# Scores ride with first halves, and three blocks' second halves are made after the maximum

## The chip, the core and the metric

The kernel runs on one core of a Trainium2 chip. That core has a matrix engine (TensorE, PE in the profile), three elementwise engines (VectorE or DVE, ScalarE or ACT, GpSimd or POOL), a queue engine (SyncE or SP) and 16 DMA engines. Each engine runs its own instruction list in order, and waits on semaphores for the others. The metric is device time in microseconds (us), lower is better.

## The reference, cut to what matters

Two graph layers over 2048 rows of 512 features, each followed by a residual and a layer norm. The first layer adds `adj @ x` with a few corrections for pairs of rows. The second is the one the change touches:

```python
seq = (x @ W_seq).reshape(N, 16, 32)                  # N = 2048, 16 heads of 32
score1 = einsum('nhd,d->hn', seq, a1)
score2 = einsum('nhd,d->hn', seq, a2)
scores = leaky_relu(score1[:, :, None] + score2[:, None, :], 0.2)
attn   = softmax(scores + (1 - adj) * -65500, axis=-1)
hidden = einsum('hij,jhd->ihd', attn, seq).reshape(N, 512)
x      = layernorm(x + elu(hidden @ W_out + b_out))
```

`adj` has some five ones in a row, so the softmax is taken over gathered neighbours only. It is made stable with one bound for each head: the largest `score2` of all 2048 rows.

## The kernel before

Rows are tiled into 16 blocks of 128 (`NB` = 16). The whole program is written out by hand, engine by engine; nothing reorders it. What runs when is set by the order in each engine's list and by semaphores.

**First stage (up to about 157 us).** The adjacency rows are read, cast, turned and multiplied with x.

**Middle stage (157 to 231 us).** For each block b, in a software pipeline over the engines: ScalarE lays `x * scale` in a PSUM bank (`scale_x`), TensorE adds the pair correction (`correct`), VectorE sums and measures the row (`sum_rows`), ScalarE takes the root, VectorE normalizes (`norm_rows`), TensorE turns the block (`turn_x1`), ScalarE saves it (`save_xT`), and TensorE multiplies it with W_seq in two halves (`make_seq`, L867). Each half is 256 columns of seq and 16 columns of scores: score1 (`s1`) with the first half, score2 (`s2`) with the second. ScalarE saves them (`save_seq`, L1140 the half, L1142 the scores), and SyncE stores the finished block of seq and s2 into the table `seqtab` in HBM (L491). Beside this, `spread_keys`, `save_keys` and `pick_edges` make for each row a list of up to four neighbours (`eidx`) and `one_hots` (L1915) the squares that place gathered rows.

**The turn (231 to 241 us).** With all 16 blocks' scores saved, VectorE reduces s2 to a maximum (L1967), TensorE turns it (L956), VectorE reduces and lays it on a diagonal (L1970, L1971), TensorE spreads it to all partitions (L959), and VectorE copies it out (L1976). Then come VectorE's instructions for the node's own weight and the bound (L2017 to L2043), and the first block's `arguments` (L2049 to L2057).

**Last stage (237 to 385 us).** For each block, GpSimd gathers 5 rows a node from `seqtab` (L616: one `near` and four `eidx`, 128 rows of 528 numbers each), VectorE makes the exponents' arguments, ScalarE takes Relu and Exp (L1257, L1259), VectorE lays the node's own share (`own_share`, L1999), weighs the gathered rows (`weigh`, L2080), TensorE adds them up (L985), VectorE divides (`finish`, L2010, L2012), TensorE turns and projects with W_out (L885, L894), ScalarE and VectorE do the elu, the residual and the last norm.

**What orders the gathers.** The gather's four buffers (`GR` = 4) hold one block each. GpSimd starts when the first 13 blocks (`CUT` = 13) are in the table (semaphore `tab_first`). For the first three blocks (`EARLY` = 3) the edges are sorted so that four gathers need only these 13 blocks (semaphore `e_low`) and the fifth needs the whole table (`e_high`). GpSimd's list is: 12 low gathers, wait for the whole table (`tab_store`), 3 high gathers, then 5 gathers for each of blocks 3 to 15, from block 4 on after TensorE has released the buffer (`e_agg`).

## Time and profile before

| | us |
|---|---|
| median of 3 runs (lowest, highest) | 387.03 (386.94, 387.91) |
| the profiled execution | 387.15 |
| its span, first to last instruction | 385.4 |
| busy in the span: PE, DVE, ACT, POOL | 346.7, 324.0, 201.2, 183.8 |
| mean granted TensorE clock | 0.971 |

The profiled execution's own time is 1.75 us more than its span, and 0.12 us above the median. PE is busy for 90% of the span and DVE for 84%, but these are means: PE holds the time up to 231 us, and DVE is busy in 19.3 of 20 us in the stretches after 280 us. Line numbers are those of the kernel before.

### The profile page before, as it was taken

Reading aid. Unit: us, or ns where it says so; the run is one execution under the profiler, and the core shown is the slowest. Engines: PE = TensorE matmul, PEld = TensorE weight load, DVE = VectorE, ACT = ScalarE, POOL = GpSimd, SP = SyncE. Lnnn points to the kernel's source line nnn. Section 1 sums busy time; section 2 is a strip of 40 time slices with the busy share of each in tenths; the row PEclk is TensorE's granted clock in tenths of the full one; section 3 lists DMA queues with packets and bytes.
Section 4 is the critical chain, followed back from the end, with each engine's and each line's share of the span. In section 5 each row is a group of like instructions: output and inputs, shape, how many; then the busy total and the mean of one; then the engine's idle time right before and its main releaser. Section 6 shows DMA issues by size and latency. Waiting matters only on the chain.

```text
span 385.4 us, 5301 instructions
## 1 busy us (share of the span) xinstructions
PE 346.7 (90%) x1676; PEld 218.5 (57%) x1676; DVE 324.0 (84%) x846; ACT 201.2 (52%) x453; POOL 183.8 (48%) x178
## 2 busy tenths in 40 slices
PE   0899899999999989999999992999999999999870
PEld 0444555455444454578888871786676555665540
DVE  2999999997797758777888868998999999999772
ACT  3955876545632013465555432132457776677780
POOL 7775738777773100000000077687788888750000
PEclk9999999999999999999999996699999999999995
DMA  7999553345898210681121178666666776760014
GB/s 247 371 384 381 211 189 142 112 140 170 201 228 193 95 70 0 201 321 56 57 77 66 58 192 260 193 167 169 188 184 169 205 216 194 193 191 36 27 58 145
DMA packets 34758, 65.11 MB, mean 169 GB/s; under 512 B 15648, under 2 KB 16800, under 8 KB 32672
## 3 DMA queue, kind: packets, MB, share of 16 engines
q1 hardware_dynamic: 25632, 42.45, 32.8%
q0 software_dynamic: 9088, 22.20, 21.6%
q8 instruction: 17, 0.28, 0.3%
q14 instruction: 21, 0.17, 0.1%
HBM read 53.50 MB, written 8.52 MB: 161 GB/s over the span
## 4 chain that ended last, share of the span: by engine, by line
PE 43%; DVE 36%; ACT 5%; issue 5%; POOL 5%; DMA 4%; SPq 0%; DVEq 0%; ACTq 0%; POOLq 0%
PE ps L867 14%; PE ps L664 14%; DVE adjT L2080 8%; PE ps L985 5%; POOL pr L546 5%; DMA arenaA<-in_x_dram 3%; DVE arenaC L1948 2%; DVE stage L1946 2%; DVE ps L2006 2%; DVE ps L1999 2%; DVE arenaA L2012 2%; DVE arenaB L1349 2%; PE ps L856 2%; DVE arenaB L1915 2%; PE ps L646 1%
## 5 line engine op out<-in xcount | busy, mean ns | idle before, releaser
L664 PE MATMUL ps<-arenaB,adjT 128*128 128x512 f16 x512 | 116.9, 384 | 3.1 <-ACT adjT L1045 1.9
L546 POOL DMA_INDIRECT pr<-in_adj_dram,aidx x79 | 82.2, 1040 | 32.1 <-issue 22.4
L616 POOL DMA_INDIRECT adjT<-seqtab,eidx x64 | 80.0, 1250 | 19.5 <-issue 19.5
L664 PEld LDWEIGHTS ps<-arenaB,adjT 128*128 128x128 f16 x512 | 49.6, 99 | 60.7 <-issue 4.0
L985 PE MATMUL ps<-adjT,arenaB 128*128 128x264 f32 x256 | 63.7, 398 | 1.7 <-DVE adjT L2080 1.1
L616 POOL DMA_INDIRECT adjT<-seqtab,near x16 | 15.8, 987 | 97.4 <-DMA seqtab<-arenaA 91.8
L867 PE MATMUL ps<-stage 128*128 128x272 f32 x256 | 61.5, 393 | 0.1
L985 PEld LDWEIGHTS ps<-adjT,arenaB 128*128 128x128 f32 x256 | 49.3, 196 | 18.6 <-DVE adjT L2080 5.0
L894 PE MATMUL ps<-adjT 128*128 128x512 f32 x120 | 54.0, 592 | 0.0
L867 PEld LDWEIGHTS ps<-stage 128*128 128x128 f32 x256 | 47.4, 190 | 9.4 <-ACT stage L1134 0.6
L2080 DVE TENSOR_TENSOR adjT<-adjT 128x1024 f32<-128x1024 f32 (+2 forms) x37 | 47.8, 1307 | 0.3
L1036 ACT ACTIVATE halves<-stage 128x2048 f16<-128x2048 f32 x16 | 30.8, 1923 | 14.1 <-DVE deg L1380 6.6
L894 PEld LDWEIGHTS ps<-adjT 128*128 128x128 f32 x120 | 21.6, 190 | 21.5 <-issue 21.5
L1045 ACT COPY adjT<-ps 128x1024 f16<-128x1024 f16 x20 | 19.2, 1014 | 22.7 <-PE ps L646 22.7
L1354 DVE TENSOR_TENSOR arenaA<-iota,halves 128x2048 f16<-128x2048 f16 x15 | 18.3, 1222 | 5.4 <-ACT halves L1036 5.2
L646 PE MATMUL ps<-identh,halves 128*128 128x128 f16 x176 | 13.3, 236 | 9.6 <-ACT halves L1036 9.6
L1361 DVE MAX8 arenaA<-arenaA 128x8 f16<-128x256 f16 x60 | 21.1, 414 | 0.5
L1366 DVE MAX8 arenaA<-arenaA 128x8 f16<-128x256 f16 x60 | 20.8, 409 | 0.0
L1165 ACT COPY ps<-adjT 128x512 f32<-128x512 f32 x15 | 8.9, 591 | 22.0 <-DVE stage L1946 22.0
L1140 ACT COPY arenaA<-ps 128x256 f32<-128x256 f32 x32 | 12.0, 375 | 14.4 <-PE ps L867 14.4
L646 PEld LDWEIGHTS ps<-identh,halves 128*128 128x128 f16 x176 | 12.0, 106 | 12.0 <-issue 9.1
L1257 ACT ACTIVATE stage<-stage 128x80 f32<-128x80 f32 (+2 forms) x19 | 4.8, 253 | 24.8 <-DVE stage L2057 24.8
(302 smaller groups left out, 501.9 us busy)
## 6 DMA issues: line engine op xcount, KB each, us to landing
stage<-in_adj_dram SPq DMA_DIRECT2D x16, 1024.0 KB, 5.4
seqtab<-arenaA SPq DMA_DIRECT2D x16, 264.0 KB, 2.3
arenaA<-in_x_dram SPq DMA_DIRECT2D x4, 1024.0 KB, 13.2
out_dram<-arenaC SPq DMA_DIRECT2D x16, 256.0 KB, 3.5
arenaB<-in_x_dram SPq DMA_DIRECT2D x1, 1536.0 KB, 10.6
pr<-in_adj_dram,aidx POOLq DMA_INDIRECT x79
arenaC<-in_L_gnn_Wq_dram SPq DMA_DIRECT2D x1, 1024.0 KB, 16.6
arenaC<-in_L_gnn_Wk_dram SPq DMA_DIRECT2D x1, 1024.0 KB, 19.7
```

What stands on the lines that cost most here:

```text
L546: g.indirect_dma_start(out=avals[:, t:t + 1], out_offset=None, in_=adj_flat, in_offset=bass.IndirectOffsetOnAxis(ap=aidx[:, t:t + 1], axis ...
L616: g.indirect_dma_start(out=Grow[:, b % GR, k, :], out_offset=None, in_=table, in_offset=bass.IndirectOffsetOnAxis(ap=source, axis=0)).then ...
L646: ins = t.transpose(turn_banks(b)[:, j, :], arowh[:, b % 2, j * P:(j + 1) * P], identh[:])
L664: ins = t.matmul(bank(4 + b % 2), adjT[:, b, j, :], xsplit[:, w, j, :], start=(j == 0 and w == 0), stop=(j == NB - 1 and w == 1))
L867: ins = t.matmul(half_bank(n), xT[:, b % 2, k, :], Wx[:, k, s, :], start=(k == 0), stop=(k == KT - 1))
L894: ins = t.matmul(bank(6 + b % 2), hT[:, b % 2, k, :], Wo[:, k, :], start=False, stop=(k == KT - 1), skip_group_check=True)
L985: ins = t.matmul(bank(2 * (b % 2) + c, HALF), square, Grow[:, b % GR, k, c * HALF:(c + 1) * HALF], start=False, stop=(k == GE - 1), skip_g ...
L1036: s.activation(arowh[:, b % 2, :], arow[:, b % 2, :], ACT.Identity, accum_out=deg[:, 0, b:b + 1]).then_inc(row_cast, 1)
L1045: s.copy(adjT[:, b, 8 * k:8 * k + 8, :], turn_banks(b)[:, 8 * k:8 * k + 8, :]).then_inc(row_evac, 1)
L1361: v.max(top[:, 0, 8 * k:8 * k + 8], key[:, k * SEG:(k + 1) * SEG])
L1366: ins = v.max(top[:, 0, 8 * k:8 * k + 8], key[:, k * SEG:(k + 1) * SEG])
L2080: v.tensor_tensor(some[:, :, 0:D1], some[:, :, 0:D1], some[:, :, D1:HW].to_broadcast([P, (last - first) * H1, D1]), ALU.mult).then_inc(e_m ...
```

## The change

Nothing is computed otherwise; what moves is where and when. Both score columns sit in the first half's product, which grows from 272 to 288 columns; the second half shrinks from 272 to 256. ScalarE writes the 16-bit copy of s1 (`ek`) that VectorE wrote. `sum_rows` and `correct` of a block run up to two blocks further ahead of `make_seq`. Blocks 13, 14 and 15 make their first halves one after another, and their second halves (`make_half(..., 1)`) follow, mixed with the maximum's small products. `EARLY` is 2, so that 8 low gathers stand ahead of the wait for the whole table instead of 12. The last stage begins with the low parts of blocks 0 and 1, then their high parts.

```diff
-    EARLY = 3
+    EARLY = 2
+        PARTS = [(0, 0, KE), (1, 0, KE), (0, KE, GE), (1, KE, GE)] + [(b, 0, GE) for b in range(EARLY, NB)]
...
+        def nth_half(b, k):
+            return 2 * b + k if b < CUT else 2 * CUT + k * (NB - CUT) + b - CUT
+        def keys_bank(b):
+            return ps[:, 4, 256:256 + KE * KW] if b == NB - 2 else ps[:, 7, 0:KE * KW]
+        def summed_in(b):
+            return {0: (2,), 1: (3,), 2: (4, 5), 3: (6,), 4: (7, 8)}.get(b, (b + 4,) if b + 4 < NB else ())
+        def normed_in(b):
+            return {0: (1,), 1: (2,), 2: (3,), 3: (4, 5), 4: (6,), 5: (7, 8)}.get(b, (b + 3,) if b + 3 < NB else ())
...
             for b in range(NB):
-                sp.wait_ge(seq_saved, 2 * b + 2)
-                sp.wait_ge(s12_saved, 2 * b + 2)
+                sp.wait_ge(seq_saved, nth_half(b, 1) + 1)
+                sp.wait_ge(s12_saved, 3 * b + 3)
                 sp.dma_start(seqtab[b * P:(b + 1) * P, :], rows_of[:, b, :]).then_inc(tab_first if b < CUT else tab_store, 16)
...
+            def make_half(b, half, lo=0, hi=KT):
+                n = nth_half(b, half)
+                pe.wait_ge(x_evac, b + 1)
+                if n >= 3:
+                    pe.wait_ge(seq_saved, n - 2)
+                cols = slice(SC + D // 2, SC + D) if half else slice(0, SC + D // 2)
+                for k in range(lo, hi):
+                    ins = t.matmul(half_bank(b, half), xT_of(b)[:, k, :], Wx[:, k, cols], start=(k == 0),
+                                   stop=(k == KT - 1))
...
+            def save_half(b, k):
+                act.wait_ge(seq_made, nth_half(b, k) + 1)
+                made = half_bank(b, k)
+                if k == 0:
+                    s.copy(s1[:, b, :], made[:, 0:H1]).then_inc(s12_saved, 1)
+                    s.copy(ek[:, b, 18:18 + H1], made[:, 0:H1]).then_inc(s12_saved, 1)
+                    s.copy(s2[:, b, :], made[:, H1:SC]).then_inc(s12_saved, 1)
+                    made = made[:, SC:]
+                s.copy(seq[:, b, 8 * k:8 * k + 8, 0:D1], made.rearrange("p (h d) -> p h d", h=8)).then_inc(seq_saved, 1)
...
+            def save_last():
+                save_half(CUT + 2, 1)
+                save_keys(CUT + 1)
+                save_keys(CUT + 2)
...
                         if n == 1:
+                            act.wait_ge(tab_first, 16 * CUT)
+                            s.copy(s2[:, 0:CUT], ones[:, 0:1].unsqueeze(1).to_broadcast([P, CUT, H1])).then_inc(self_exp, 1)
                             act.wait_ge(self_made, 1)
                             s.activation(sa[:, 2], sa[:, 1], ACT.Exp).then_inc(self_exp, 1)
+                            save_last()
+                        if b == 4:
+                            table_stored(act)
+                            s.copy(s2[:, CUT:], ones[:, 0:1].unsqueeze(1).to_broadcast([P, NB - CUT, H1])).then_inc(self_exp, 1)
...
+                    dve.wait_ge(e_low[0], 16 * KE)
+                    arguments(0, 0, KE)
+                    self_rest()
+                    one_hots(3)
+                    self_parts()
+                    own_share(0)
+                    weigh(0, 0, KE)
+                    dve.wait_ge(e_low[1], 16 * KE)
+                    arguments(1, 0, KE)
+                    own_share(1)
+                    weigh(1, 0, KE)
+                    dve.wait_ge(e_high[0], 16)
+                    arguments(0, KE, GE)
+                    one_hots(4)
+                    weigh(0, KE, GE)
+                    dve.wait_ge(e_high[1], 16)
+                    arguments(1, KE, GE)
+                    one_hots(5)
+                    weigh(1, KE, GE)
+                    finish(0)
```

TensorE's list at the end of the middle stage, before. L867 is a half of seq (4 products), L877 the keys, L956 and L959 the maximum, L929 a product that opens a PSUM bank:

```order
L867 MATMUL ps<-stage 128x272 [waits s12_saved,x_evac]
L867 MATMUL ps<-stage 128x272 x3
L867 MATMUL ps<-stage 128x272 [waits s12_saved]
L867 MATMUL ps<-stage 128x272 x3
L877 MATMUL ps<-ekb,stage 128x51 [waits keys_saved,s1_split,span_made]
L877 MATMUL ps<-ekb,stage 128x51 x3
L877 MATMUL ps<-ekb,stage 128x51 [waits keys_saved,s1_split,span_made]
L877 MATMUL ps<-ekb,stage 128x51 x3
L956 MATMUL ps<-ident,gm 16x128 [waits g_part]
L959 MATMUL ps<-gm,ones 128x16 [waits keys_saved,g_diag]
```

And now, from the middle of block 13's second half (L887 a half, L904 the keys, L989 and L993 the maximum, L956 a bank):

```order
L989 MATMUL ps<-ident,gm 16x128 [waits g_part]
L887 MATMUL ps<-stage 128x256 [waits seq_saved,x_evac]
L887 MATMUL ps<-stage 128x256
L887 MATMUL ps<-stage,halves 128x256 [waits seq_saved,x_evac]
L993 MATMUL ps<-gm,ones 128x16 [waits g_diag]
L887 MATMUL ps<-stage,halves 128x256 [waits seq_saved,x_evac]
L887 MATMUL ps<-stage,halves 128x256 x2
L904 MATMUL ps<-ekb,stage 128x51 [waits keys_saved,s1_split,span_made]
L904 MATMUL ps<-ekb,stage 128x51 x3
L956 MATMUL ps<-iota,identh 128x512 x2
L887 MATMUL ps<-stage 128x256 [waits seq_saved,x_evac]
```

Both products of the maximum stood behind all halves; now ten of the twelve products of the last three second halves stand behind the first of them, and block 15's second half stands last.

ScalarE's list at the turn, before (L1142 the last scores, L1150 keys, L1257 and L1259 the first block's Relu and Exp):

```order
L1142 COPY arenaA<-ps 128x16
L1150 CAST halves<-ps 128x204 [waits keys_spread] x2
L296 TENSOR_LOAD badi [waits flag_made]
L296 ISA x2
L1248 COMPARE_AND_BRANCH
L1249 ACT_TABLE_LOAD
L1257 ACTIVATE stage<-stage 128x64 [waits e_arg]
L1259 ACTIVATE adjT<-stage 128x64 [waits e_cap]
L1262 ACTIVATE arenaB<-arenaB 128x256 [waits self_made]
```

And now (L1191 a half of seq, L1203 keys, L1328 and L1330 Relu and Exp):

```order
L1308 ACT_TABLE_LOAD
L1191 COPY arenaA<-ps 128x8x32 [waits seq_made] x2
L1203 CAST halves<-ps 128x204 [waits keys_spread]
L296 TENSOR_LOAD badi [waits flag_made]
L296 ISA x2
L1321 COMPARE_AND_BRANCH
L1328 ACTIVATE arenaB<-arenaB 128x64 [waits e_arg]
L1330 ACTIVATE adjT<-arenaB 128x64 [waits e_cap]
L1333 COPY arenaA<-ones 128x208 [waits tab_first]
L1335 ACTIVATE arenaB<-arenaB 128x256 [waits self_made]
L1191 COPY arenaA<-ps 128x8x32 [waits seq_made]
L1203 CAST halves<-ps 128x204 [waits keys_spread] x2
```

The copy of block 15's second half, on which the last store to the table waits, stood ahead of the first block's Relu; now it stands behind that block's Exp, a fill of ones and the own weights' Exp.

## Rows read from the trace of the kernel before

**Rows 1.** The chain of waits, 225 to 275 us: start us, length us, what.
```profile
231.23 0.60 DVE gm L1967
...
241.21 7.51 PE ps L985 x20
...
249.16 4.45 PE ps L985 x20
...
262.37 4.45 PE ps L985 x20
```

**Rows 2.** TensorE in order of time: start us, length us, engine, line.
```profile
213.69 0.38 PE L848 MATMUL ps<-scores,arenaA 128*128 128x512 f16 x1
213.91 0.60 PE L856 MATMUL ps<-ident,arenaC 128*128 128x128 f32 x4
214.34 3.83 PE L867 MATMUL ps<-stage 128*128 128x272 f32 x16
218.01 0.26 PE L877 MATMUL ps<-ekb,stage 128*128 128x51 f16 x4
```

**Rows 3.** ScalarE in order of time, from the last stores to the first weights.
```profile
218.21 0.37 ACT L1140 COPY arenaA<-ps 128x256 f32<-128x256 f32 x1 [0.69 <-PE ps L867]
218.48 0.19 ACT L1142 COPY arenaA<-ps 128x16 f32<-128x16 f32 x1
...
237.51 0.26 ACT L1257 ACTIVATE stage<-stage 128x64 f32<-128x64 f32 x1 [3.74 <-DVE stage L2057]
237.80 0.32 ACT L1259 ACTIVATE adjT<-stage 128x64 f32<-128x64 f32 x1
238.18 0.42 ACT L1262 ACTIVATE arenaB<-arenaB 128x256 f32<-128x256 f32 x1
```

**Rows 4.** GpSimd in order of time; in brackets the idle time before and its releaser.
```profile
222.27 0.95 POOL L616 DMA_INDIRECT adjT<-seqtab,near  x1 [91.77 <-DMA seqtab<-arenaA]
...
232.51 0.94 POOL L616 DMA_INDIRECT adjT<-seqtab,near  x1 [0.30 <-issue]
...
249.49 0.95 POOL L616 DMA_INDIRECT adjT<-seqtab,near  x1 [1.35 <-PE ps L985]
...
253.51 1.97 POOL L616 DMA_INDIRECT adjT<-seqtab,eidx  x1 [0.31 <-issue]
...
263.42 0.94 POOL L616 DMA_INDIRECT adjT<-seqtab,eidx  x1 [0.30 <-issue]
```

**Rows 5.** VectorE in order of time; L2049 begins a block's arguments.
```profile
229.71 0.42 DVE L1910 TENSOR_TENSOR arenaB<-halves 128x256 f32<-128x256 f16 x1
...
236.70 0.27 DVE L2049 TENSOR_TENSOR stage<-arenaB,adjT 128x64 f32<-128x64 f32 x1
...
256.58 0.29 DVE L2049 TENSOR_TENSOR stage<-arenaB,adjT 128x80 f32<-128x80 f32 x1
...
262.64 0.30 DVE L2049 TENSOR_TENSOR stage<-arenaB,adjT 128x80 f32<-128x80 f32 x1
...
269.07 0.69 DVE L1946 SCALAR_TENSOR_TENSOR stage<-ps,adjT 128x512 f32<-128x512 f32 x1 [1.08 <-ACT adjT L1176]
...
270.41 0.29 DVE L2049 TENSOR_TENSOR stage<-arenaB,adjT 128x80 f32<-128x80 f32 x1
...
280.15 0.29 DVE L2049 TENSOR_TENSOR stage<-arenaB,adjT 128x80 f32<-128x80 f32 x1
```

**Rows 6.** Line L616, 236 to 270 us: the gathers' landing.
```profile
DMA to landing us min/median/max: 3.4/4.0/4.8
```

**Rows 7.** Line L491, 200 to 222 us, then 226 to 236 us: the stores' landing.
```profile
DMA to landing us min/median/max: 2.0/2.0/2.8
...
DMA to landing us min/median/max: 4.0/4.1/4.3
```

**Rows 8.** Stretches: length; busy us of PE, PEld, DVE, ACT, POOL; granted clock; DMA share.
```profile
233.00:234.00 1.00, 1.00 (x5) 0.48 (x5) 0.75 (x3) 0.77 (x1) 0.70 (x2) 0.64 0.89 340
...
247.00:248.00 1.00, 1.00 (x6) 0.86 (x5) 1.00 (x2) 0.00 (x0) 0.85 (x1) 1.00 0.75 199
```

More of the change, by code:

```diff
@@ L313, in table_stored, with lots_of @@
             eng.wait_ge(tab_store, 16 * (NB - CUT))
-        def lots_of(b):
-            if b == 0:
-                return tuple((k, k + 1) for k in range(GE))
-            return ((0, 2), (2, KE), (KE, GE)) if b < EARLY else ((0, 2), (2, GE))
+        def lots_of(b, lo):
+            if b >= EARLY:
+                return ((0, 2), (2, GE))
+            if lo:
+                return ((KE, GE),)
+            return ((0, 2), (2, KE)) if b else tuple((k, k + 1) for k in range(KE))
+        LOTS = [(b, first, last) for b, lo, hi in PARTS for first, last in lots_of(b, lo)]
         def weighed(b, k):
-            before_b = sum(len(lots_of(a)) for a in range(b))
-            return before_b + 1 + [lo <= k < hi for lo, hi in lots_of(b)].index(True)
+            return [a == b and first <= k < last for a, first, last in LOTS].index(True) + 1
         def bank(n, width=512):
@@ L357, in two_layer_graph_attention @@
         x1 = ax
-        HC = D // 2 + H1
-        Wx = part(stage, 0, [KT, 2, HC])
+        SC = 2 * H1
+        Wx = part(stage, 0, [KT, SC + D])
         xT = part(stage, 2304, [2, KT, P])
+        xT_late = part(halves, 1408, [KT, P])
         eT = part(arenaB, 0, [2, N])
@@ L383, in two_layer_graph_attention @@
         mxe = part(arenaB, NB * GE * H1, [NB, GE * H1])
-        span = part(stage, 3328, [2, KE * P], F16)
+        span = part(stage, 3328, [3, KE * P], F16)
         spare = adjbuf
@@ L388, in two_layer_graph_attention @@
         ehot = part(arenaB, 3840, [HOTS, KE, P])
-        earg = part(stage, 2 * KE * P, [3, GE * H1])
+        earg = part(arenaB, 3840 + HOTS * KE * P, [3, GE * H1])
         sden = sb("sden", [P, 2, H1])
@@ L966, in pe_second_layer @@
                 with pe.If(misfit < 1):
[L967 to L968 removed]
+                    for b, lo, hi in PARTS:
+                        if (b, lo) == (0, KE):
+                            pe.wait_ge(keys_saved, NB)
                             open_bank(6)
@@ L1228, in act_first_norm @@
                 scale_x(2)
-                for b in range(NB):
-                    if b + 3 < NB:
-                        scale_x(b + 3)
+                for b in range(CUT):
+                    ahead = summed_in(b + 1)
+                    late = b in (2, 4)
+                    if not late:
+                        for c in ahead[0:1]:
+                            scale_x(c)
                     if b == 0:
                         save_xT(0)
-                    if b + 1 < NB:
-                        root(b + 1)
+                    for c in normed_in(b):
+                        root(c)
                     if b >= 1:
                         save_xT(b)
-                    if b >= 1:
                         save_seq(b - 1)
@@ L2075, in weigh @@
                         dve.wait_ge(e_exp, nth_part(b, lo))
-                        for first, last in lots_of(b):
-                            if not lo <= first < hi:
-                                continue
+                        for first, last in lots_of(b, lo):
                             some = G[:, b % GR, first * H1:last * H1]
```

230 lines of the change are left out of this document (120 added, 110 removed).

## The prediction, made before the changed kernel was run

> **What bounds the kernel now.** I read the chain of waits first, because it says which engine holds the time at each stage. Up to 231 us it lies on TensorE, whose blocks follow each other without a gap. At 231.23 us VectorE's maximum takes over. From 241.21 us the chain shows TensorE's sums, twenty products in 7.51 us where later blocks take 4.45 [rows 1]. After 269 us it lies on VectorE to the end.
>
> Then I read VectorE in order of time for that last part. The first arguments start at 236.70 us, block 3's at 256.58, block 4's at 262.64, block 5's at 270.41 and block 6's at 280.15. The only idle time of note is 1.08 us at 269.07 [rows 5]. So today the last part is VectorE's own work, 33.7 us from the first arguments to block 5's.
>
> Last I read GpSimd, which nobody seems to wait for. It starts at 222.27 us, its ninth gather starts at 232.51, so one takes 10.24 / 8 = 1.28 us, and the last gather of block 5 starts at 263.42 [rows 4]. A gather lands 4.0 us after its issue in this stretch (3.4 to 4.8) [rows 6]. So block 5 is complete at about 267.4 us and VectorE asks for it at 270.41. The slack is only 3.0 us, and that number decides this change.
>
> **The maximum, and with it the last stage, starts earlier.** Two halves of a block take 218.01 - 214.34 = 3.67 us, a correction 0.22 (213.69 to 213.91) and a turn 0.43 (213.91 to 214.34), starts compared [rows 2]. Block 12 ended at 218.01. Now one more correction and one more turn lie ahead of its end, +0.65: 218.66. Block 15's turn and two key products follow (0.43 + 2 x 0.10), then three first halves of 288 columns, each 3.67 x 288 / 544 = 1.94 us. They end at 225.1. ScalarE's copy started 0.2 us after the product (218.21 against 218.01) and three small copies take some 0.4, from 0.19 each and overlapping [rows 3]. With VectorE's last 16-column maximum it is 225.9 us, where it was 231.83 (231.23 + 0.60) [rows 1].
>
> From there to the first arguments it took 236.70 - 231.83 = 4.87 us. Now VectorE has four small instructions of the neighbour list and the keys ahead, 0.17 to 0.42 us each as at 229.71 [rows 5], some 0.9 in all, and the two small products queue behind two or three products of a second half, for which I add 0.4. That makes 6.2 us: first arguments at 232.1, 4.6 us earlier. The extra cast on ScalarE (0.19 each) has cover, since ScalarE waits for TensorE in every block (0.69 at 218.21 [rows 3]). The fill of ones leaves VectorE for ScalarE; on VectorE it was hidden behind ScalarE's Exp, so I count nothing for it there. `sum_rows` run ahead cost VectorE nothing in total; they fill it earlier. Without that cover, TensorE would stand in the middle stage, which is a rival below.
>
> **The gathers start a little later and then stand.** Block 12's store went out after 218.67 (218.48 + 0.19), and GpSimd started at 222.27, 3.6 us later [rows 3, 4]. Now its half is saved at 218.66 + 0.2 + 0.37 = 219.23, and without a score copy behind it counts at once. GpSimd starts at 222.8, about 0.5 later. Eight gathers end its free work at 233.0. The ninth waits for the whole table, and that waits for block 15's second half.
>
> TensorE has that half ready at about 232.5: from 225.1 three second halves of 1.73 (3.67 x 256 / 544) give 5.2, two opened banks 0.9, the rest is small products and the wait for the diagonal. But ScalarE takes it only after the first block's Exp. Before, the Relu started 0.81 us after the arguments, the Exp 0.29 later and the own weights' Exp 0.38 after that, ending 1.90 after the arguments' start [rows 3, 5]. With the fill of ones between (0.3, a copy of less width than the Exp's 0.42) and a half's 0.27 to 0.37, the half is saved at 232.1 + 1.9 + 0.3 + 0.3 = 234.6. Add the 3.6 of block 12's store: GpSimd goes on at 238.2 us. It has stood 5.2 us. The ninth gather was at 232.51, so it is 5.7 us late. Stores land in 2.0 to 2.8 us there and in 4.0 to 4.3 beside gathers [rows 7], so the 3.6 may be 0.8 too much or 2.3 too little.
>
> GpSimd gets back 1.05 us: before block 4 it waited 1.35 for TensorE where the ordinary step is 0.30 [rows 4], and TensorE will be done with block 0 by then. So block 5's last gather is 5.7 - 1.05 = 4.6 us late.
>
> **The sum.** VectorE alone would ask for block 5 at 232.1 + 33.7 - 1.08 = 264.7, 5.7 us earlier than today. But the gather lands at 263.42 + 4.6 + 4.0 = 272.0, which is 1.6 us later than the 270.41 of today. The 4.6 us gained at the turn are waited away: first 3 to 4 us at block 2, whose fifth gather starts six steps of 1.28 after 238.2 and lands at 249.9, while VectorE is there by about 246 (232.1, and 13.8 for two blocks: the 19.9 from 236.70 to 256.58 for three, less the 6.1 of one); the rest at blocks 3 to 5. Behind block 5 VectorE bounds again, since block 6 was asked for only at 280.15, 9.7 us later, and GpSimd needs some 7.5 a block (below). So 1.6 us stays to the end: 387.15 + 1.6 = 388.75 us for the profiled execution, which was 0.12 above the median of the runs. I say 388.6.
>
> One unknown is how long a gather takes beside VectorE. The gather at 253.51 took 1.97 us instead of 0.95 [rows 4], while VectorE weighed block 2. The ten gathers of blocks 4 and 5 took from 249.49 to 264.36, 14.9 us or 7.5 a block, where ten steps of 0.95 + 0.30 are 12.5. Between none of this and twice this lies -2.4 to +2.4 at block 5; I take the same as today, because the same weighing of blocks 2 to 4 falls on the same gathers.
>
> The landing is the other term with weight. The Trainium skill (DMA: Bandwidth & Descriptors, "Anatomy of one DMA") fits a transfer issued from GpSimd as 2.0 us plus bytes over 436 GB/s. For 270 KB that would be an estimated 2.6 us, and block 5 would be complete 1.4 us earlier, which leaves 0.2 us of loss. No gather of this stretch lands under 3.4 [rows 6], so the measurement decides.
>
> **The rivals.** (a) Faster, 385.2 us. The gathers catch up. VectorE idles some 5 us between blocks 1 and 5, and GpSimd's steps in that time are clean 1.25s. For it: the clean steps before 236 us. Against it: every weighing still takes place while gathers run. Price: 238.2 + 21 x 1.25 = 264.5, landed at 268.5, a gain of 1.9: 387.15 - 1.9 = 385.25, or 385.1 on the median's scale. It decides for faster as soon as block 5's last gather starts before 265.2 us, a gain of more than 1.2. The Trainium skill (SBUF — State Buffer, "SBUF: two separate sides") speaks for this rival: GpSimd's descriptor writing is locked out only while a VectorE instruction holds the port pair they share, so a waiting VectorE stretches nothing. The trace agrees as far as the 1.97 goes; no run shows yet how much of the stretch the waits remove.
>
> (b) No change, 387.0 us. ScalarE or the store is 1.6 us quicker than I have it, for instance a store that lands in 2.0 us because GpSimd's queue is empty. For it: 2.0 in the quiet stretch. Against: block 12's 3.6 us were already quiet.
>
> (c) Slower still, 390.8 us. TensorE becomes the second bound. Its clock fell at 233.0 to 234.0 (0.64 granted on average, on the way from 2.4 to 1.2 GHz) when it had little to do, and was back at 247.0 [rows 8], so block 0 and its neighbours took 7.51 instead of 4.45. If the wait for block 2 makes it fall again, block 2's sums run slow, 3 us late. I work out that they end near 260, block 3's at 268.5, while VectorE wants these at about 269: covered by half a microsecond. If not covered, or if the corrections run ahead make TensorE stand earlier, it is 2 us more.
>
> (d) That the change doesn't do what it says: the maximum still ends near 231, because the first halves wait for banks. Then nothing is gained at the turn, and the store is later by the same amount: about 389 to 392. I give it little.
>
> **How the numbers follow.** Forecast 0.55, (a) 0.20, (b) 0.15, (c) and (d) 0.10. What can't be told from no change is 0.3%, 1.2 us. The forecast's own range is 387.3 to 389.9, with half of the gathers' stretch and of the store's bounds. Faster: (a) and a little of (b), 0.22. Same: most of (b) and 0.07 of the forecast, 0.20. Slower: 0.58. The range reaches from 385.3 to 390.6.
>
> **What would show it.** In the profile after: first halves ahead of the maximum and VectorE's first arguments near 232 (right if 231 to 233.5). GpSimd idle for 4 to 6 us before its ninth gather, released by the stores, ending near 238. VectorE idle about 3 us before block 2's arguments and some more at blocks 3 to 5, released by gathers. Block 5's arguments near 272, and from there on the same distances as before, 9.7 us to block 6. ScalarE's copy of the last half near 234.5. The prediction is wrong if GpSimd's idle time is under 3 us, if VectorE does not wait for block 5, or if block 5's arguments start before 270.4.

## The result: 0.2 to 0.45% slower, and the profile after

The changed kernel took 388.23 us (median of 20 runs, 386.55 to 391.7) against 386.94 for the kernel before: a ratio of 1.0045, 95% interval 1.003 to 1.0059. A second series gave 387.89 and 1.0017 (0.9997 to 1.0037), which alone would not tell it from no change, and the kernel before against itself 0.9999 (0.9979 to 1.0019). The forecast was 388.6. The profiled execution took 388.47 us, its span 386.7.

The two profiled executions can't be laid over each other by their clocks, because the stage ahead of the projection ended 1.7 us earlier in one. So I count from the first product of the projection. In the rows of before it is this one (timeline: start, us, engine, line), and then the one of after:

```profile
160.37 3.94 PE L867 MATMUL ps<-stage 128*128 128x272 f32 x16
```

```profile
158.69 3.50 PE L887 MATMUL ps<-stage 128*128 128x288 f32 x14
```

From here on "at 70.0" means 70.0 us behind that product. The kernel before, profiled a second time, shows how well this repeats: first arguments at 76.33 both times, block 5's at 110.04 and 110.15, block 6's at 119.78 and 119.85.

VectorE of after, in order of time, answers to [rows 5]:

```profile
224.00 0.19 DVE L2028 TENSOR_TENSOR gm<-gm,arenaA 128x16 f32<-128x16 f32 x1 [0.84 <-ACT arenaA L1189]
...
228.71 0.27 DVE L2139 TENSOR_TENSOR arenaB<-arenaB,adjT 128x64 f32<-128x64 f32 x1
...
235.37 0.28 DVE L2139 TENSOR_TENSOR arenaB<-arenaB,adjT 128x64 f32<-128x64 f32 x1 [1.01 <-DMA adjT<-seqtab,eidx]
...
239.98 0.19 DVE L2139 TENSOR_TENSOR arenaB<-arenaB,adjT 128x16 f32<-128x16 f32 x1 [0.79 <-DMA adjT<-seqtab,eidx]
...
249.13 0.30 DVE L2139 TENSOR_TENSOR arenaB<-arenaB,adjT 128x80 f32<-128x80 f32 x1 [4.62 <-DMA adjT<-seqtab,eidx]
...
255.87 0.31 DVE L2139 TENSOR_TENSOR arenaB<-arenaB,adjT 128x80 f32<-128x80 f32 x1 [1.35 <-DMA adjT<-seqtab,eidx]
...
262.61 0.30 DVE L2139 TENSOR_TENSOR arenaB<-arenaB,adjT 128x80 f32<-128x80 f32 x1 [0.58 <-DMA adjT<-seqtab,eidx]
...
269.89 0.69 DVE L2036 SCALAR_TENSOR_TENSOR stage<-ps,adjT 128x512 f32<-128x512 f32 x1 [1.30 <-ACT adjT L1229]
...
271.23 0.30 DVE L2139 TENSOR_TENSOR arenaB<-arenaB,adjT 128x80 f32<-128x80 f32 x1
...
280.93 0.29 DVE L2139 TENSOR_TENSOR arenaB<-arenaB,adjT 128x80 f32<-128x80 f32 x1
```

The maximum is done at 224.19 (65.5), and the first arguments start at 70.0, where they were at 76.3: the turn came 6.3 us forward. Then the waits for gathers eat it: 1.01 us ahead of block 1's low part, 0.79 ahead of block 0's high part, 4.62 at block 2, 1.35 at block 3, 0.58 at block 4. The first of these is not from GpSimd standing, since block 1's low gathers are issued before it stands, and the second profile below doesn't have it. Block 5's arguments are at 112.5 and block 6's at 122.2, 2.4 us later than before.

GpSimd of after answers to [rows 4]:

```profile
220.22 0.94 POOL L636 DMA_INDIRECT adjT<-seqtab,near  x1 [91.41 <-DMA seqtab<-arenaA]
...
229.58 1.07 POOL L636 DMA_INDIRECT adjT<-seqtab,eidx  x1 [0.30 <-issue]
236.32 1.27 POOL L636 DMA_INDIRECT adjT<-seqtab,eidx  x1 [5.67 <-DMA seqtab<-arenaA]
...
244.74 0.95 POOL L636 DMA_INDIRECT adjT<-seqtab,eidx  x1 [0.31 <-issue]
...
265.51 2.50 POOL L636 DMA_INDIRECT adjT<-seqtab,eidx  x1 [0.30 <-issue]
```

It starts at 61.5 (before 61.9) and stands 5.67 us ahead of its ninth gather. The last row is block 5's last gather, at 106.8. It landed 5.6 us later, at 112.4, just ahead of block 5's arguments at 112.5. ScalarE of after answers to [rows 3]; the fifth row is the last half's save:

```profile
229.53 0.26 ACT L1328 ACTIVATE arenaB<-arenaB 128x64 f32<-128x64 f32 x1 [1.20 <-DVE arenaB L2147]
229.82 0.32 ACT L1330 ACTIVATE adjT<-arenaB 128x64 f32<-128x64 f32 x1
229.98 0.55 ACT L1333 COPY arenaA<-ones 128x208 f32<-128x208 f32 x1
230.32 0.42 ACT L1335 ACTIVATE arenaB<-arenaB 128x256 f32<-128x256 f32 x1
230.64 0.36 ACT L1191 COPY arenaA<-ps 128x256 f32<-128x256 f32 x1
```

And the chain of waits of after shows what lies behind the save, where [rows 1] had the maximum:

```profile
231.03 5.03 DMA seqtab<-arenaA
...
236.32 1.27 POOL adjT L636
...
244.74 4.36 DMA adjT<-seqtab,eidx
...
252.10 7.15 PE ps L1027 x20
```

TensorE stood 6.77 us ahead of block 2's sums, and its granted clock went to the lower of its two levels (0.50 of 2.4 GHz, so 1.2), as in [rows 8]. The twenty products took 7.15 us. The windows of after (PE, PEld, DVE, ACT, POOL busy, clock, DMA share, GB/s):

```profile
248.00:250.00 2.00, 0.00 (x0) 0.00 (x0) 0.80 (x4) 0.00 (x0) 1.39 (x3) 1.00 0.73 222
250.00:252.00 2.00, 0.00 (x0) 0.00 (x0) 1.92 (x4) 1.52 (x4) 1.70 (x2) 0.56 0.82 220
252.00:254.00 2.00, 1.90 (x5) 1.52 (x6) 1.97 (x3) 0.00 (x0) 1.70 (x2) 0.50 0.44 156
258.00:260.00 2.00, 2.00 (x12) 1.55 (x11) 2.00 (x2) 0.28 (x1) 1.39 (x3) 1.00 0.79 220
```

### The profile page after: what moved, and what is told of

Its sections match the earlier page's. It is cut to its first block, busy times and chain, and to the rows that moved or that the text cites. A ratio compares the mean times of both kernels' runs of the same rounds, so it can differ in the third digit from the quotient of the medians.

```text
span 386.7 us, 5313 instructions
## 1 busy us (share of the span) xinstructions
PE 347.4 (90%) x1676; PEld 219.0 (57%) x1676; DVE 319.8 (83%) x823; ACT 201.8 (52%) x469; POOL 184.2 (48%) x178
## 4 chain that ended last, share of the span: by engine, by line
DVE 36%; PE 33%; POOL 10%; issue 7%; DMA 6%; ACT 5%; SPq 0%; DVEq 0%; ACTq 0%; POOLq 0%
PE ps L887 13%; POOL pr L566 9%; DVE adjT L2166 8%; PE ps L684 8%; PE ps L1027 3%; DVE arenaB L1427 3%; DMA arenaA<-in_x_dram 3%; DVE arenaC L2038 2%; DVE stage L2036 2%; DVE ps L2096 2%; DVE arenaA L2102 2%; DVE ps L2089 2%; PE ps L876 2%; DVE arenaB L1992 2%; POOL adjT L636 1%
## 5 line engine op out<-in xcount | busy, mean ns | idle before, releaser
L636 POOL DMA_INDIRECT adjT<-seqtab,eidx x64 | 76.2, 1190 | 24.9 <-issue 19.2
L1027 PE MATMUL ps<-adjT,arenaB 128*128 128x264 f32 x256 | 65.0, 403 | 2.2 <-DVE adjT L2166 1.5
L636 POOL DMA_INDIRECT adjT<-seqtab,near x16 | 20.6, 1288 | 96.0 <-DMA seqtab<-arenaA 91.4
L887 PE MATMUL ps<-stage 128*128 128x288 f32 (+1 forms) x240 | 58.0, 393 | 0.1
L887 PEld LDWEIGHTS ps<-stage 128*128 128x128 f32 x240 | 44.3, 190 | 9.2 <-ACT stage L1180 0.6
L1328 ACT ACTIVATE arenaB<-arenaB 128x80 f32<-128x80 f32 (+2 forms) x18 | 4.6, 255 | 28.3 <-DVE arenaB L2147 28.3
L1191 ACT COPY arenaA<-ps 128x256 f32<-128x256 f32 x32 | 12.1, 393 | 10.8 <-PE ps L887 10.8
```

What stands on the lines that cost most here:

```text
L636: g.indirect_dma_start(out=Grow[:, b % GR, k, :], out_offset=None, in_=table, in_offset=bass.IndirectOffsetOnAxis(ap=source, axis=0)).then ...
L887: ins = t.matmul(half_bank(b, half), xT_of(b)[:, k, :], Wx[:, k, cols], start=(k == 0), stop=(k == KT - 1))
L1027: ins = t.matmul(bank(2 * (b % 2) + c, HALF), square, Grow[:, b % GR, k, c * HALF:(c + 1) * HALF], start=False, stop=(k == GE - 1), skip_g ...
```

## The experiments

Twelve runs, of 6 to 12 executions each. The table has the medians, the ratio to the kernel before, and from the profile the start of block 5's and block 6's arguments behind the first product. That start tells smaller effects apart than the median does, whose ratio is known to 0.2 or 0.3%. But each position comes from one or two profiled executions, and where a gather sets it, it moves with that gather's landing, by 0.3 us between the two profiles of the changed kernel.

```
                                      median   ratio (95%)             block 5   block 6
before, first profile                 386.94   -                       110.04    119.78
before again                          386.73   0.9999 (0.9979-1.0019)  110.15    119.85
changed                               388.23   1.0045 (1.003-1.0059)   112.54    122.24
changed again                         387.89   1.0017 (0.9997-1.0037)  112.23    121.94
before, two split                     387.95   1.0030 (1.001-1.0049)   110.39    120.08
before, two split, again              387.46   1.0018 (1.000-1.0035)   110.50    120.20
changed, three split                  384.45   0.9930 (0.9911-0.9948)  109.63    119.32
changed, last half first              387.93   1.0032 (1.0004-1.006)   111.44    121.13
changed, late half                    387.98   1.0032 (1.0008-1.0056)  111.70    121.40
changed, busy                         386.76   1.0004 (0.9985-1.0024)  111.33    121.02
three split + last half first         384.34   0.9950 (0.9924-0.9976)  108.20    117.90
the same, two gathers fewer           383.87   0.9917 (0.9886-0.9948)  108.10    117.84
the same, busy                        384.32   0.9941 (0.9917-0.9965)  108.04    117.75
the same, busy, two gathers fewer     383.24   0.9901 (0.987-0.9932)   106.48    116.21
```

**Three split blocks in the changed kernel.**

```diff
-    EARLY = 2
+    EARLY = 3
-PARTS = [(0, 0, KE), (1, 0, KE), (0, KE, GE), (1, KE, GE)] + [...]
+PARTS = [(0, 0, KE), (1, 0, KE), (2, 0, KE), (0, KE, GE), (1, KE, GE), (2, KE, GE)] + [...]
+SUMMED = [(0, 0, KE), (1, 0, KE), (0, KE, GE), (1, KE, GE), (2, 0, KE), (2, KE, GE)] + [...]  # TensorE
...
+                    dve.wait_ge(e_low[2], 16 * KE)
+                    arguments(2, 0, KE)
+                    weigh(2, 0, KE)
...
```

> The changed kernel, with the gathers of block 2 split as well, as they were before the change: twelve gathers of low rows stand ahead of GpSimd's wait for the whole table instead of eight, and block 2's low part is weighed before the high parts of blocks 0 and 1. Theory T (the loss comes from GpSimd standing for the whole table behind only eight gathers): four more gathers of 1.28 us fill 5.1 of the 5.67 us; GpSimd idles under 1 us there, VectorE's 4.62 us wait ahead of block 2 goes, block 5 is asked for some 4 us earlier, and the time is about 384 us, 0.8% under the kernel before (3 us), 4 under the changed one. Rival M (the new middle stage, or the order of the parts, costs what is gained): the time stays at 387.5 to 388.5. Rival V (VectorE's own work is the bound from block 3 on and the wait was covered): within 1 us of the changed kernel.

Measured: 384.45 us, 0.7% under the kernel before. So theory T holds in its main point and both M and V fall: the early scores do pay, once GpSimd has work in front of its wait. Block 5 came 2.9 us earlier, where T had said 4. GpSimd still idles 2.23 us, not under 1, because the last store now lands in 6.80 us (chain, then GpSimd's and VectorE's timeline):

```profile
231.19 6.80 DMA seqtab<-arenaA
```

```profile
238.26 1.95 POOL L638 DMA_INDIRECT adjT<-seqtab,eidx  x1 [2.23 <-DMA seqtab<-arenaA]
```

```profile
239.93 0.27 DVE L2141 TENSOR_TENSOR arenaB<-arenaB,adjT 128x64 f32<-128x64 f32 x1 [0.54 <-DMA adjT<-seqtab,eidx]
...
254.03 0.30 DVE L2141 TENSOR_TENSOR arenaB<-arenaB,adjT 128x80 f32<-128x80 f32 x1 [2.04 <-DMA adjT<-seqtab,eidx]
...
268.51 0.30 DVE L2141 TENSOR_TENSOR arenaB<-arenaB,adjT 128x80 f32<-128x80 f32 x1 [1.25 <-DMA adjT<-seqtab,eidx]
```

Of the wait ahead of block 2 0.54 us is left. A wait of 2.04 us stands ahead of block 3, and block 5 now waits for its own gather, 1.25 us.

**The kernel before with two split blocks**, twice.

```diff
-    EARLY = 3
+    EARLY = 2
...                                  # one_hots stay with the blocks they were with
```

> The kernel before, with only the number of split blocks taken from 3 to 2; the scores, the maximum and the parts stand where they stood. Theory T: GpSimd's eight gathers end at 232.5 us, the last store lands near 235, so GpSimd stands some 2.5 to 3 us; it had 3.0 us of slack at block 5 and gets 1.05 back at block 4, and the first arguments stay at 236.7. So the time is that of the kernel before to within 0.5 us (386.6 to 387.6): the split alone costs next to nothing, and only beside the earlier maximum is it the limit. Rival S (fewer split blocks cost by themselves, about as much as the whole change): 388.3 or more. Rival C (the lower instruction count of VectorE for block 2 helps): 386 or less.

> The kernel before with only two split blocks, once more: its median was 1.003 of the kernel before (1.001 to 1.0049), while its profile put block 6's arguments only 0.3 us later than the kernel before does, counted from the projection's first product (120.08 against 119.78 and 119.85). If the trace is right and the first series was high by chance, the ratio is 1.000 to 1.002 and block 6 stands at 120.0 to 120.4 again. If fewer split blocks cost 1 us by themselves, the ratio is 1.002 to 1.004, and the second profile shows VectorE's wait for block 4's gathers (1.89 us in the first) longer, block 6 at 120.8 or more.

GpSimd stood 3.09 and 3.24 us, as T has it, and block 5 came 0.3 to 0.4 us later:

```profile
236.51 0.96 POOL L616 DMA_INDIRECT adjT<-seqtab,eidx  x1 [3.24 <-DMA seqtab<-arenaA]
```

```profile
265.39 0.32 DVE L2049 TENSOR_TENSOR stage<-arenaB,adjT 128x80 f32<-128x80 f32 x1 [1.95 <-DMA adjT<-seqtab,eidx]
```

Block 6 came at 120.08 and 120.20, the second inside the 120.0 to 120.4 of "the trace is right"; VectorE's wait for block 4's gathers was 1.89 and 1.95 us, so it did not grow. The medians say more, 1.3 and 0.6 us against the runs of before in the same series, and T's 386.6 to 387.6 missed the first. Some 0.35 us of both lies outside the span: a run of this kernel takes 2.18 and 2.15 us more than its span (medians), one of the kernel before 1.81. Why is open, and so is the rest of the first. So the split alone costs 0.3 us by the trace and 0.6 to 1.3 by the clock. With the early scores it costs 2.9 at block 6 (122.24 against 119.32) and some 3.6 us of time. The two parts of the change are not additive: the early scores without the smaller split gain 2.2 us (384.45 against 386.66 in the same series), the smaller split alone loses 0.6 to 1.3, both together lose 1.0 to 1.3.

One thing in these profiles bears on the whole case. Block 5's last gather starts at 106.5 here, where the changed kernel has it at 106.8 and 106.0. Here it landed in 3.9 us, at 110.4, and there in 5.6 and 6.25. So at block 5 the changed kernel is no longer behind in when it issues that gather, but in how long that gather takes.

**The last half first.**

```diff
+                make_half(CUT + 2, 1)          # behind block 14's, ahead of keys and banks
                 spread_keys(CUT)
...
-                make_half(CUT + 2, 1)
...
                 save_half(CUT + 1, 1)
+                save_half(CUT + 2, 1)          # was behind the first Exp
                 save_keys(CUT)
...
-                save_half(CUT + 2, 1)
```

> The changed kernel, with block 15's second half made right behind block 14's on TensorE (ahead of the keys and two opened banks) and saved by ScalarE ahead of the first Relu, not behind the first Exp, the fill of ones and the own weights' Exp. Theory T: the half is saved 1.2 to 1.7 us earlier, GpSimd's idle time falls from 5.67 to about 4.3 us, and the gathers and VectorE's wait ahead of block 2 follow one for one; block 5 is not set by its gather any more in the changed kernel's trace, so the end moves by 1 to 1.5 us: about 387.0. Rival V (the wait is covered by VectorE's own bound): 388.2, unchanged. Rival M (moving keys and banks costs at the first arguments): slower than the changed kernel.

The half was saved 1.2 us earlier, GpSimd's idle time fell to 3.50 us, and block 6 came 1.1 us earlier than in the first profile of the changed kernel, 0.8 earlier than in the second:

```profile
234.49 1.44 POOL L636 DMA_INDIRECT adjT<-seqtab,eidx  x1 [3.50 <-DMA seqtab<-arenaA]
```

The sign is T's. But the gathers did not follow one for one: the ninth came 2.2 us earlier than in the first profile (75.5 against 77.6), block 5's last only 0.4 (106.4 against 106.8). The median moved by 0.3 us only, which the noise covers, so by the time nothing is shown. The changed kernel's second profile, with 4.63 us of idle time and nothing changed, shows how far the store's landing varies by itself.

**The last half late.**

```diff
+    s.copy(zt.rearrange("p a d -> p (a d)"), iota[:, 0:2 * D]).then_inc(opened_late, 1)
+    s.copy(ze.rearrange("p a d -> p (a d)"), iota[:, 0:2 * D]).then_inc(opened_late, 1)
+    act.wait_ge(opened_late, 2)
     save_last()
```

> The changed kernel, with two copies of 1024 columns into unused scratch on ScalarE ahead of block 15's last save: some 2 us more before the last store, and nothing else of that stage waits for them. Theory T: GpSimd stands 7.7 us instead of 5.67, VectorE waits 2 us longer ahead of block 2, and the time is 1.7 to 2.2 us more than the changed kernel's, about 390.2. Rival V: under 0.5 us more. It gives the slope of the end against the stall, together with the kernel that saves the half early.

T failed here. The save came 2.0 us later (235.41 in a run whose first product was at 161.43, so 74.0, where it was 72.0), but GpSimd went on at 77.2 instead of 77.6:

```profile
235.41 0.37 ACT L1192 COPY arenaA<-ps 128x256 f32<-128x256 f32 x1
```

```profile
238.64 1.26 POOL L637 DMA_INDIRECT adjT<-seqtab,eidx  x1 [5.23 <-DMA seqtab<-arenaA]
```

The last store landed in 2.6 us instead of 5.03. (The expectation under "Three split, last half first" calls it 2.9, which was the median of the last three stores.) In the changed kernel's two profiles and the busy kernel's below it was issued at 72.3 each time and landed at 77.4, 76.3 and 76.1; issued at 74.4 here, it landed at 77.0, and at 71.2 with the last half first, at 75.2. So the save 2 us later brought the landing no later than the changed kernel's own spread. This fits a store that waits behind the data of the eight gathers just ahead of it: with 2.4 us for them to drain it took half of 5.03. No run looked at the store's own data, so that reason is argued and not shown. Rival V's "under 0.5 us more" came out, though not by V's cause: the stall that the edit was to lengthen did not grow.

**TensorE kept busy** in its gap ahead of block 2's sums.

```diff
...
     turn_hidden(b - 2)
+    if b == 2:
+        for _ in range(28):
+            t.matmul(bank(5), identh[:], iota[:, 0:512], start=True, stop=True)
...
```

> The changed kernel, with 28 more products of 512 columns on TensorE into a bank that nobody reads, behind the turn of block 0's hidden rows, in the gap in which TensorE waits for block 2 (6.77 us there). They keep the granted clock at its upper level and leave all else where it stands. Theory C (the part of the loss that GpSimd's wait does not explain is TensorE's clock, which falls to the lower level in this gap: block 2's twenty sums take 7.15 us instead of 4.45 and the elu of block 0, for which VectorE waits 1.30 us ahead of block 5, is late by that): block 2's sums take some 4.5 us, the wait of 1.30 goes, block 5 is asked for at about 111.2 us behind the first product of the sequence's projection instead of 112.54, and the time falls by 1.0 to 1.5 us to about 387. Rival G (block 5's gather, which ended its landing just before, sets it anyway): at most 0.4 us.

```profile
244.29 6.21 PE L1018 MATMUL ps<-iota,identh 128*128 128x512 f16 x28
250.83 1.13 PE L1030 MATMUL ps<-adjT,ident 128*128 128x264 f32 x4 [0.33 <-DVE adjT L2169]
251.80 3.72 PE L1030 MATMUL ps<-adjT,arenaB 128*128 128x264 f32 x16
```

The sums took 4.69 us (250.83 to 255.52), the wait for the elu is gone, block 5 came at 111.33 and the median was 386.76: the numbers are theory C's. Shown is that GpSimd's wait makes the gap, that the clock falls in it, and that unused products hold it up. That the gain at block 5 comes from the clock is not shown. In both profiles of the changed kernel block 5's last gather landed at 112.4 and 112.2, so without the wait for the elu VectorE would have waited for that gather to within 0.1 us of the same time. In the busy kernel the gather started at 106.5 and landed in 4.5 us, at 111.0; what set block 5 there was VectorE's own work behind its wait at block 4:

```profile
262.97 0.30 DVE L2142 TENSOR_TENSOR arenaB<-arenaB,adjT 128x80 f32<-128x80 f32 x1 [2.57 <-DMA adjT<-seqtab,eidx]
```

And the two kernels with slow sums whose gather landed in 5.0 and 4.7 us, last half first and late half, had block 5 at 111.44 and 111.70 without any busy products. So rival G's mechanism, the gather, stands beside C's, and this run can't tell them apart.

**Three split, last half first.** Both edits from above.

> The kernel with three split blocks, and block 15's second half made right behind block 14's and saved ahead of the first Relu. Theory Q (the last store is held up behind the data of the gathers issued ahead of it: it landed in 2.9 us when issued last, 5.0 behind eight gathers, 6.8 with twelve): issued 1 us earlier, with fewer gathers ahead of it, it lands some 2 us earlier, so that GpSimd's 2.23 us of idle time ahead of its 13th gather goes to under 1 and block 5, which is set by its own gather there, is asked for 1 to 1.5 us earlier: about 383.3 us, under the kernel with three split blocks (384.45). Rival F (what the store gains, the gathers that share the DMA engines with it lose): no change against that kernel, 384.4.

The store landed in 4.0 us and GpSimd does not idle at all between its first gather and block 6. Block 5 came 1.4 us earlier than with three split alone, as Q said; the median, 384.34 against 384.45, doesn't show it, and Q's 383.3 was missed. In the three kernels below, whose store is issued at the same place, it landed in 5.1, 5.2 and 3.7 us, so a part of what it gained against 6.80 is the landing's own spread.

**Two gathers fewer, and TensorE busy, on that kernel.**

```diff
-                    for k in range(GE):
+                    for k in range(b in (4, 5), GE):      # two gathers fewer
                         gather(b, k, e_gather[b % GR])
...
-                        dve.wait_ge(e_gather[b % GR], 16 * GE * ((b - EARLY) // GR + 1))
+                        dve.wait_ge(e_gather[b % GR], 16 * (GE * ((b - EARLY) // GR + 1) - (b % GR < 2)))
...
                             open_bank(7)
+                            for _ in range(12):           # busy
+                                t.matmul(bank(5), identh[:], iota[:, 0:512], start=True, stop=True)
```

> The kernel before this in the list (three split blocks, last half first), which leaves out the gathers of the nearest neighbours of blocks 4 and 5 (two of GpSimd's gathers; their slots keep old rows, VectorE's and TensorE's work is the same). Theory G (from the first arguments on, GpSimd's gathers set when block 5 can be weighed, not VectorE): block 5's last gather starts 2.5 us earlier and lands 2.5 earlier, block 5 is asked for earlier by what VectorE waits for gathers at blocks 4 and 5, 1 to 1.6 us, and the end moves by the same: some 382.2. Rival V (VectorE's own work): no change, under 0.3 us.

> The kernel with three split blocks and the last half first, with twelve more products on TensorE into an unread bank ahead of the high parts' sums, where TensorE stands 3.06 us and its clock then runs at the lower level for some 4 us (in the trace of the kernel with three split blocks). Theory C: the eight sums behind it take 2 us instead of 3.85 and GpSimd's next slots come free earlier, but block 5 is set by its gather and not by TensorE: within 0.4 us of the same kernel without them. If the clock mattered there, 1 us less.

> Three split blocks, last half first, the twelve products that keep TensorE's clock up, and the gathers of the nearest neighbours of blocks 4 and 5 left out. Each of the last two by itself left block 5's arguments at 108.0 to 108.1 us behind the first product: without the two gathers VectorE waited 1.30 us for the elu of block 0, behind TensorE's slow sums; with the products it waited 1.35 for its gather. Theory D (two bounds stand one behind the other, gathers and TensorE, at the same place): both together give 1 to 1.3 us, arguments at 106.8 to 107.1, and some 383 us. Rival V (VectorE's own work stands right behind both): under 0.4 us.

The kernels with fewer gathers leave out two neighbours and so compute something else; they only price the gathers. Alone, neither edit moved block 5: 108.20 became 108.10 and 108.04. G's 1 to 1.6 us was wrong, though its first half held: block 5's last gather started 2.9 us earlier (100.8 against 103.7), although GpSimd stood 2.19 us for block 4's buffer, which TensorE had to release. What VectorE waited for changed, as its rows show, of the kernel with fewer gathers, of the busy one, and of the one with both:

```profile
267.39 0.69 DVE L2038 SCALAR_TENSOR_TENSOR stage<-ps,adjT 128x512 f32<-128x512 f32 x1 [1.30 <-ACT adjT L1231]
```

```profile
266.94 0.31 DVE L2143 TENSOR_TENSOR arenaB<-arenaB,adjT 128x80 f32<-128x80 f32 x1 [1.35 <-DMA adjT<-seqtab,eidx]
```

```profile
264.34 0.69 DVE L2040 SCALAR_TENSOR_TENSOR stage<-ps,adjT 128x512 f32<-128x512 f32 x1 [1.30 <-ACT adjT L1233]
...
265.67 0.33 DVE L2143 TENSOR_TENSOR arenaB<-arenaB,adjT 128x80 f32<-128x80 f32 x1
```

Together they gave 1.6 us at block 5 and 1.1 in the median, a little more than D's 1 to 1.3. The eight sums of the high parts show where it came from, with fewer gathers and with both:

```profile
248.00 3.62 PE L1029 MATMUL ps<-adjT,arenaB 128*128 128x264 f32 x8 [2.87 <-DVE adjT L2168]
```

```profile
245.99 2.21 PE L1031 MATMUL ps<-adjT,arenaB 128*128 128x264 f32 x8
```

They start at 87.4 and 86.8, so 0.6 of the 1.6 us was there before the faster sums and is not shown to be the edit's: VectorE was already 1.25 us ahead at block 2's low part, when the products had not run yet. The remaining 1.0 fits the clock, with sums that are 1.4 us shorter. The kernel that both start from is a poor partner for this: in its profile the clock had not fallen (its gap was 2.58 us, the mean granted clock 1.00 from 242 to 250 us), so there the twelve products had nothing to hold up. With this said, D stands: gathers and TensorE's sums with the elu behind them bound block 5 at nearly the same time. Even the last kernel, whose sums are all fast, waits 1.30 us for the elu.

**Both kernels once more.**

> The kernel before, unchanged, once more: a second profile, and a ratio of the kernel against itself. The stage ahead of the projection differs between executions by when the last pair gather lands (3.2 to 5.4 us behind its issue in the profiles so far, the projection's first product at 158.4 to 161.4 us). If that is noise that both kernels share, the first product's time comes out anywhere in that stretch here, while the distance from it to the span's end is 225.0 us to within 0.5, and to block 6's arguments 119.8 to within 0.3. The ratio is 1.000 to within 0.2%.

> The changed kernel, unchanged, once more. The distance from the projection's first product to the first arguments is 70.0 us again (before 76.3). The store of block 15 landed in 5.03 us in the first profile, where kernels that differ little showed 2.9 to 4.0. If the 5.03 was on the long side, GpSimd's idle time is 4 to 5 us here and block 6's arguments stand 121.2 to 122.0 us behind the first product, not 122.24; if it is the rule behind eight gathers, 5.5 to 5.8 us and 122.2 again. The ratio is 1.003 to 1.006.

The kernel before came out as expected: first product at 160.49, block 6 at 119.85, the span's end 225.5 us behind the first product (225.0 the first time), a ratio of 0.9999. Of the changed kernel, the first arguments (70.0), the idle time (4.63 us) and block 6 (121.94) are in their ranges; the ratio, 1.0017, is under the 1.003 to 1.006 expected.

Ahead of block 5 the second profile of after shows the gather, not the elu, as the last to come:

```profile
265.05 6.25 DMA adjT<-seqtab,eidx
```

```profile
271.32 0.30 DVE L2139 TENSOR_TENSOR arenaB<-arenaB,adjT 128x80 f32<-128x80 f32 x1 [0.82 <-DMA adjT<-seqtab,eidx]
```

The gather landed 6.25 us after it began. GpSimd's idle time was 4.63 us, so the 5.67 was on the long side, and yet block 6 was only 0.3 earlier.

## Why the prediction was right, and where it was not

The forecast was a loss of 1.6 us from GpSimd standing for the whole table. The sign came out, and the time, 388.23 and 387.89 against 388.6, lies in the range. The first half of the mechanism came out too: the turn gains, GpSimd stands, and with twelve gathers ahead of the wait 3.6 us of time come back. How the loss then arises at block 5 was in part another way than said, and that the total still fits is in part luck. Step by step, positions counted from the first product (at 160.37 in the rows of before):

- The maximum: 225.9, so 65.5. Measured 65.5.
- The turn: 6.2 us, first arguments at 71.7. Measured 4.5 us and 70.0. The small instructions for which I added 0.9 and 0.4 fell into VectorE's waits.
- GpSimd's start: 222.8, so 62.4. Measured 61.5, since block 12's store landed in 2.0 us, not in the 2.8 of before.
- The last half's save: done at 234.6, so 74.2. Measured 72.3, with the turn 1.7 of the difference.
- From the save to the ninth gather: 3.6 us, "0.8 too much or 2.3 too little". Measured 5.3 and 4.3, of which the store's landing is 5.03 and 3.99. The 3.6 held block 12's landing of 2.8, so by [rows 7] the bounds were 0.8 too much or 1.5 too little. The ninth gather, said to be at 77.8, came at 77.6 and 76.6. Two errors cancelled, an earlier save and a slower store. The late half experiment suggests that they do so in part by themselves, since there the later save had the faster store.
- GpSimd idle 5.2 us. Measured 5.67 and 4.63.
- Block 2's wait: 3 to 4 us. Measured 4.62 and 4.89. In the first profile VectorE was there at 85.8, nearly as said (85.5), because its two waits ahead of blocks 1 and 0 took back what the turn had gained more, and the gather landed at 90.4, not 89.5. In the second VectorE was there 0.7 us sooner than said.
- GpSimd's pace: the same as before. From the ninth to block 5's last gather there are 21 steps: 29.19 us, 1.39 each (1.40 in the second profile), against 1.42 of before without its one wait. Rival (a) needed 1.25 and falls in its size. The Trainium skill (SBUF — State Buffer, "SBUF: two separate sides") has a waiting VectorE stretch nothing, and the trace agrees: while VectorE waits ahead of block 2, GpSimd's rows at 244.74 to 248.49 are all 0.95 long. But the stretched ones come elsewhere, up to 2.50 us at 265.51: of the 22 gathers from the ninth to block 5's last, 7 took over 1.05 us, where it was 6 of 22 before. (The 14.9 us of two blocks held ten gathers but nine steps between them, so "none of this" is 2.7 us off and not 2.4.)
- What rival (a) had right shows only over all the kernels with two split blocks. With one exception, the longer GpSimd stood, the less its gathers were stretched behind it. What gathers nine to 29 took over 0.95 us each adds up to 5.3 and 5.2 us behind idle times of 3.09 and 3.24, 4.6 behind 3.50, 3.8 behind 4.41, 3.1 behind 4.63, 3.4 behind 5.23 and 2.9 behind 5.67. So the ninth gather lies anywhere from 74.8 to 77.6 in these seven profiles, and block 5's last only from 106.0 to 107.0. A stall that was 2.6 us longer moved block 5's last gather by 1 us at most. That the waiting VectorE is the reason fits, but no run tried it by itself.
- Block 5's arguments: 111.6, set by the gather. Measured 112.54 and 112.23. This is the step that was mis-sized. The last gather began earlier than said (106.8 and 106.0, not 107.7) but landed in 5.6 and 6.25 us instead of 4.0. In the second profile VectorE waited 0.84 for the elu and then 0.82 for the gather. In the first it waited 1.30 for the elu of block 0 and found the gather landed 0.1 us before, so by the prediction's own sign, "wrong if VectorE does not wait for block 5", this profile speaks against it, if only by that 0.1. TensorE, which I had "covered by half a microsecond", was not covered: rival (c)'s mechanism took place beside the forecast's. But the gather came no earlier, so by these two profiles it cost at most 0.1 us at block 5, and not 2 more. Why this one gather lands so late stays open; it landed in 3.9 us in both two-split versions of the kernel before, where its writing took 0.95 and 1.01 us, and in 4.5 to 6.25 in the five profiles with early scores and two split blocks, where its writing took 1.45 to 2.50 us.
- From block 5 to block 6: 9.7. Measured 9.70.

So at block 6 the loss behind the first product was 2.1 to 2.5 us, not 1.6. The medians show 1.3 and 1.0. The difference lies ahead of the projection: the first product came at 160.37 and 160.49 in the kernel before (159.32 and 161.50 in its two-split versions), and at 158.4 to 161.4, median 159.0, in ten profiles with the changed stage. There VectorE waits, now longer and now shorter, for the last pair gather (1.84 us in before's profile, 0.52 in after's). Whether that is chance or a side effect of the edit was not tried. The total is right in part because this half of the error points the other way, and that is luck: nothing in the prediction has it.

## What to carry to other kernels

When a change brings an engine's work forward, write down the rate of the queue that feeds it and the time of its next hard wait: here 1.4 to 1.5 us a gather and one wait for the whole table, and the 6.3 us gained at the turn were worth nothing until that queue had twelve items ahead of its wait instead of eight. Don't bundle an edit that gains with one that spends the same slack: the same change with block 2 still split makes 384.45 us where before and after take 386.9 and 388.2. And a wait that goes may only uncover a second one of equal length; look up when each of the other releasers came, even those that the profile does not name, before promising its price.

## What the runs showed of the hardware

- How long a store of a block (264 KB by the profile) takes depends on the gathers around it: 2.0 to 2.2 us ahead of all gathers of the changed kernels, 2.6 us when the last gather's writing had ended 2.4 us earlier, 3.7 to 5.03 with eight gathers issued just ahead and none behind (six profiles), 3.7 to 6.80 in the five kernels that issued four more meanwhile.
- A gather's time from its start to its landing reached 6.5 us (the eighth gather with two gathers fewer) and 6.25 at block 5, where the median of [rows 6] is 4.0. GpSimd had needed 1.45 us for the second instead of 0.95. A single gather's writing took up to 2.52 us, and the mean step from the ninth gather to the thirtieth, waits left out, lay between 1.39 and 1.51 us in all fourteen profiles, where a clean one is 1.25.
- TensorE's granted clock was at the lower level behind its gaps of 5.8 to 7.1 us in eight profiles, behind the 3.06 us gap of the three-split kernel and behind the 2.87 us gap of the one with two gathers fewer. Behind the 2.58 us gap of the three-split kernel with the last half first it stayed at 1.00. 28 unused products in the gap of the changed kernel held it at 1.00, and the sums behind then took 4.69 us instead of 7.15.
